# Layer-normalisation of token groups 1 to 3 moved from VectorE to GpSimd, and one subtraction per group moved the other way, in a fused cross-attention and mixture-of-experts kernel

## What is computed

```
x = x + attention(ctx, layernorm(x), Wq)          # causal, keys = values = ctx @ Wq.T
n = layernorm(x)                                  # the "second normalisation"
cw = top-2 of softmax(n @ gate_W), renormalised   # weights per token and expert
ffn = n
for e in range(8):
    ffn = ffn + cw[:, e:e+1] * (relu(n @ W1[e] + b1[e]) @ W2[e] + b2[e])
x = x + ffn
```

## Time and profile before

| | |
|---|---|
| median of 3 runs | 131.92 us (131.65 to 132.03) |
| the profiled execution | 130.83 us, of which the span from first to last instruction is 129.0 us |
| TensorE busy | 120.3 us, 93% of the span |
| VectorE busy | 107.6 us, 83% |
| ScalarE busy | 93.5 us, 73% |
| GpSimd busy | 53.5 us, 41% |
| granted TensorE clock | 1.0 (2.4 GHz) throughout |

### The profile page before, as it was taken

The page is one execution under the profiler, slowest core; times in us unless marked ns, Lnnn a source line. Parts: engine busy times, 40 slices in busy tenths (PEclk is TensorE's granted clock), DMA queues, the critical chain, the costliest instruction groups (busy, mean ns, idle before and its releaser), DMA issues. The chain is left out here.

```text
span 129.0 us, 3295 instructions
## 1 busy us (share of the span) xinstructions
PE 120.3 (93%) x1175; PEld 90.7 (70%) x1175; DVE 107.6 (83%) x419; ACT 93.5 (73%) x191; POOL 53.5 (41%) x57
## 2 busy tenths in 40 slices
PE   6987788999979999999999999999999979999991
PEld 2585566777847768778768778778776757776690
DVE  0629998989999999989898999958998798866683
ACT  3337485999776955996779927993799467989830
POOL 7199155330094951330095640330468303345400
PEclk9999999999999999999999999999999999999999
DMA  3999900000000000200000000200000002000002
GB/s 92 321 283 321 289 26 8 0 0 0 5 0 0 0 5 3 81 0 5 0 0 5 0 3 13 68 5 0 3 0 8 0 0 86 3 0 0 5 0 81
DMA packets 9904, 5.54 MB, mean 43 GB/s; under 512 B 504, under 2 KB 9888, under 8 KB 9888
## 3 DMA queue, kind: packets, MB, share of 16 engines
q1 hardware_dynamic: 9744, 5.27, 15.2%
q10 hardware_dynamic: 144, 0.07, 0.2%
HBM read 4.28 MB, written 1.05 MB: 41 GB/s over the span
## 5 line engine op out<-in xcount | busy, mean ns | idle before, releaser
L690 POOL TENSOR_TENSOR h_lo<-h,h_hi 128x512 f16<-128x512 f32 x24 | 28.7, 1196 | 40.2 <-ACT h L571 39.9
L571 ACT ACTIVATE h<-psH,b1T 128x512 f32<-128x512 f32 x64 | 43.3, 689 | 1.1 <-PE psH L508 0.9
L570 ACT ACTIVATE h_hi<-psH,b1T 128x512 f16<-128x512 f32 x48 | 33.0, 688 | 11.5 <-PE psH L387 11.4
L864 DVE SCALAR_TENSOR_TENSOR acc<-psY,weight_y,acc 128x128 f32<-128x128 f32 x125 | 35.1, 342 | 1.4 <-PE psY L408 1.2
L383 PE MATMUL psH<-x_hi,w_hi 128*128 128x512 f16 x62 | 23.5, 379 | 1.0 <-ACT h L571 1.0
L387 PE MATMUL psH<-x_lo,w_hi 128*128 128x512 f16 x62 | 23.5, 379 | 0.0
L384 PE MATMUL psH<-x_hi,w_lo 128*128 128x512 f16 x62 | 23.5, 379 | 0.0
L848 DVE TENSOR_TENSOR h_lo<-h,h_hi 128x512 f16<-128x512 f32 x24 | 16.5, 689 | 7.8 <-ACT h L571 7.3
L408 PE MATMUL psY<-w_hi,h_hi 128*128 128x128 f16 x192 | 22.7, 219 | 0.0
L408 PE MATMUL psY<-w_lo,h_hi 128*128 128x128 f16 x192 | 22.7, 219 | 0.0
L408 PEld LDWEIGHTS psY<-w_hi,h_hi 128*128 128x128 f16 x192 | 15.3, 98 | 2.2
(11 more groups left out here) (191 smaller groups left out, 191.4 us busy)
## 6 DMA issues: line engine op xcount, KB each, us to landing
w_sb<-in_L_ffn_W_dram SPq DMA_DIRECT2D x8, 256.0 KB, 4.9
out_dram<-acc SPq DMA_DIRECT2D x3, 256.0 KB, 2.3
x_sb<-in_x_dram SPq DMA_DIRECT2D x2, 256.0 KB, 4.0
ctx_sb<-in_ctx_dram SPq DMA_DIRECT2D x2, 256.0 KB, 4.4
x_sb<-in_x_dram SPq DMA_DIRECT2D x1, 512.0 KB, 7.6
ctx_sb<-in_ctx_dram SPq DMA_DIRECT2D x1, 512.0 KB, 8.5
out_dram<-acc SPq DMA_DIRECT2D x2, 128.0 KB, 1.8
wq_sb<-in_L_xattn_Wq_dram ACTq DMA_DIRECT2D x1, 64.0 KB, 2.8
```

The lines of the kernel that those rows point to most:

```text
L570: nc.scalar.activation(h_hi[:, C * (e % 2) + c, :], psH[c][:, :], ACT.Relu, bias=bias, scale=scale)
L571: nc.scalar.activation(h[:, C * (e % 2) + c, :], psH[c][:, :], ACT.Relu, bias=bias, scale=scale).then_inc(h_ready, 1)
L690: nc.gpsimd.tensor_tensor(h_lo[:, i, :], h[:, i, :], h_hi[:, i, :], ALU.subtract).then_inc(hlo0_ready, 1)
L864: last = nc.vector.scalar_tensor_tensor(out=o, in0=y, scalar=weight_y[:, g % 2, t, e:e + 1], in1=o, op0=ALU.mult, op1=ALU.add)
```

## The change

The second normalisation of groups 1 to 3 leaves VectorE's list of steps and goes into GpSimd's, directly behind the power. GpSimd no longer subtracts for expert 4 in groups 0 to 2 of the loop; VectorE takes that 128x512 subtraction ahead of its own for the same expert. TensorE waits for a count of GpSimd's remainders that fits.

```diff
+    DVE_PAIR = 4
...
+    def pool_takes(g, e):
+        return is_split(g, e) and not (e == DVE_PAIR and g < GROUPS - 1)
+
+    def pool_splits(g, e):
+        return sum(pool_takes(j, i) for j in range(g) for i in range(E)) + sum(pool_takes(g, i) for i in range(e + 1))
...
                     pe.wait_ge(hlo_ready, splits(g, e))
-                    pe.wait_ge(hlo0_ready, splits(g, e))
+                    pe.wait_ge(hlo0_ready, pool_splits(g, e))
...
             def hidden_lo0(g, e):
 
-                if is_split(g, e):
+                if pool_takes(g, e):
...
+            def loop_norm(a):
+                pool.wait_ge(rstd2_ready, (a + 1) * TG)
+                for t in range(TG):
+                    nc.gpsimd.tensor_scalar(xf[:, t, :], x1[:, t, :], mv2[:, t, 0:1], rstd2[:, t:t + 1],
+                                            ALU.subtract, ALU.mult).then_inc(xf_ready, 1)
+
+            steps = [(FIRST_RSTD, 2, first_rstd), (RSTD, 1, lambda a: attention_rstd(a, ALL)), (NORM2, 1, loop_norm),
+                     (BASE, 1, base_sum)]
...
             def hidden_lo(g, e):
+                if is_split(g, e) and not pool_takes(g, e):
+                    i = C * (e % 2)
+                    dve.wait_ge(h_ready, (g * E + e) * C + 1)
+                    nc.vector.tensor_tensor(h_lo[:, i, :], h[:, i, :], h_hi[:, i, :], ALU.subtract)
                 if is_split(g, e):
...
-                     (RESIDUAL, 1, residual_step), (VARIANCE, 1, variance_step), (NORM2, 1, lambda a: second_norm(a, ALL)),
+                     (RESIDUAL, 1, residual_step), (VARIANCE, 1, variance_step), 
```

More of the change, by code:

```diff
@@ L691, in hidden_lo0 @@
                                             ALU.subtract).then_inc(hlo0_ready, 1)
-            steps = [(FIRST_RSTD, 2, first_rstd), (RSTD, 1, lambda a: attention_rstd(a, ALL)), (BASE, 1, base_sum)]
+            def loop_norm(a):
[5 more added lines that the diff above has]
+                     (BASE, 1, base_sum)]
             def group(g):
```

## The result

The changed kernel took 133.65 us (median of 4 runs, 133.53 to 134.35) against 131.78 us for the kernel before measured with it (131.64 to 132.03): a ratio of 1.0162, interval 1.0102 to 1.0222. It is slower by about 1.6%, where no change was forecast. The time lies inside the stated range, at its dear end.

The account below looks back on a forecast made before the run. TensorE was taken to bound the kernel. Terms +0.45 (g = 0) - 0.06 - 0.06 (g = 1, 2) = +0.33 us on the median 131.92 gave 132.2 us, called no change (131.6 if GpSimd keeps the port); range 131.2 to 133.9.

Parts of the forecast that it names:

- The bound: TensorE sets the pace in the loop; at most 0.87 us of its waits can go; VectorE's saving is worth nothing by itself.
- Expert 4: TensorE's wait for the remainder of expert 4: 0.45 us gained in g = 0, 0.06 each in g = 1 and 2.
- I take 0.45: Price in us of one GpSimd normalisation: a quarter of the 128x512 tensor_scalar plus some 0.08; four cost 1.8.
- The affine select: GpSimd's 128x128 instruction nearest in shape, 0.29 us, taken to show 128 columns can be done well under half a microsecond.
- The bounds: Limits for one normalisation on GpSimd: 0.29 us (affine select of 128x128) and 1.50 us (tensor_scalar of 128x512).
- g = 1 and g = 2: GpSimd's series ends at 67.7, before TensorE loads `xf` from 68.14; expert 5's remainder just in time; -0.06 us each.
- The dear rival: GpSimd's normalisation costs 0.55 us or more; at 0.6 TensorE waits at the transposes, +1.9 us, 133.8; chance 0.32.
- g = 0: VectorE's subtraction and weight split delay GpSimd's fourth normalisation; TensorE waits 1.2 us instead of 0.75, +0.45 (-0.2 if GpSimd keeps the port).
- The cheap rival: GpSimd's normalisation costs 0.2 to 0.3 us, near the affine select; nothing is lost, gain 0.57 us, 131.3; chance 0.2.
- The third rival: VectorE's two subtractions do not hold up GpSimd's tensor_scalar, so the series runs early: 131.3; counted into a chance of 0.2.

Follow-up runs that it names:

- normalisation only: Changed kernel, but GpSimd keeps its subtraction for expert 4, ahead of its four normalisations; ratio to before 1.034.
- later power, two wide: Kernel before with GpSimd's power behind its kept expert 4 subtraction, and the normalisation as two 128x512 tensor_tensor on GpSimd; ratio to before 1.0094.
- the pair alone: Changed kernel with the normalisation back on VectorE, which still takes both expert 4 remainders in groups 0 to 2; ratio to before 0.998.
- constants: Changed kernel whose four GpSimd normalisations use 0.5 and 2.0 in place of each partition's mean and power; ratio to before 1.0055.
- two wide: Changed kernel with GpSimd's four tensor_scalar replaced by two tensor_tensor of 128x512 on all four tiles; ratio to before 1.0084.
- The durations run: Kernel before plus a series of GpSimd instructions behind its last subtraction, written to unread tiles; the change's form took 0.79 us at 128 columns.
- run with 32 columns: Changed kernel in which each of GpSimd's four normalisations writes 32 of the 128 columns; ratio to before 1.0051.

## Why the prediction was wrong

**The bound.** TensorE sets the pace: right. VectorE's time is worth nothing by itself: right only as long as VectorE is not late at the gate. Its busy time hardly moved (107.6 to 108.0 us), and the two kernels that take work from it (normalisation only; later power, two wide) still lose; but 0.14 to 1.55 us went at the gate in g = 0, to its `x_lo`, in seven of the ten other kernels of the table, and most of the gain of the pair alone went to its chain.

**Expert 4.** -0.45 us in g = 0 forecast, -0.48 measured, with 0.25 us of wait left where 0.3 was forecast; five other kernels with the pair have 0.47 to 0.49, constants 0.40, and two wide loses 0.35 instead, since GpSimd gets in between. In g = 1 and 2 about the forecast 0.06 came at the remainder, and 0.05 of it was gone again at the next hidden product, which waits for ScalarE.

**The step that failed** is "I take 0.45" for one normalisation on GpSimd. It took 0.79 to 0.80 undisturbed. I had scaled a tensor_scalar of one operation and a constant by columns and added 0.08 for the fixed part. The durations run gives 0.20 for the fixed part of that form and 0.27 for the second operation and its scalars. The affine select, from which I argued for a small fixed part, is no neighbour in kind. The bounds held it (0.29 to 1.50); the choice between them decided the sign, and the text itself said that 0.5 us was the point from which it does.

**g = 1 and g = 2.** With 0.45 nothing is lost, with the real price 0.65 each. The run with 32 columns, 0.46 us each, confirms the first (nothing lost in either). The dear rival, worked at 0.6 us, gave 0.4 a group; the measured 0.65 came at 0.79. TensorE waits at the transposes, as that rival said, and then 0.17 us more for the remainder of expert 5, which the rival did not have.

**g = 0.** +0.45 forecast for the group, +1.34 measured: the order of events was right (VectorE comes in behind the second normalisation; it was forecast behind the third, and the first is held up by 0.75), the length was not. The forecast also made VectorE wait for the normalisation in progress, and it did not (0.68 us at 39.32). And a step was missing even at 0.45: VectorE held up by GpSimd's postponed subtractions, late with `x_lo`, 0.87 us at the gate in the run with 32 columns. With the forecast's price and this step the sum would have been +1.2, and the run with those conditions gave +1.03. The right price alone, by the forecast's own scheme, is dearer still (worked under the rivals). So either error alone takes the forecast out of what it called no change.

**The rivals.** The cheap rival, 131.3, is excluded by the price. The dear one named the mechanism, the place and nearly the time (133.8); it had a chance of 0.32 and should have had more, for the reasons that stood beside it. That the time came so near is luck. Its scheme lets VectorE's subtraction for expert 5 in ahead of the fourth normalisation in g = 1, for about 0.6 us, where the rows show 0.08. Worked with the real 0.79 it gives, as an estimate, about +1.8 in g = 0 (the fourth `xf` ends at 42.36 against 40.57) and +1.2 in each of the others (69.66 against 68.49), some 4.1 us in all against 2.6 in the traces: a price too low and an interruption too many cancelled. The third rival, a tensor_scalar that VectorE's pair does not hold up, is wrong for the change's form (1.54 and 1.31 us for 0.79) and half right for the form with constants, which the second of the pair did not hold up. The rule of the Trainium skill (GPSIMD Engine Reference, Engine selection) of roughly line rate for one input does not hold for these instructions: 0.79 us for 128 columns, and 2.5 ns a column for the simplest form.

**Open.** Why a normalisation with scalars per partition waits for both of VectorE's subtractions, where one with constants or a tensor_tensor waits for the first only: the runs show the difference and not its cause. And how the 0.65 us of a group would split if one of its two waits were taken away without moving the other.

## What to carry to other kernels

A short instruction moved to GpSimd is priced by its own form, measured by a series at the end of the kernel: columns scaled from another form miss the fixed part, the second operation and the scalars. Before moving work off an engine that another waits for, look whether the waiting instruction merely stands behind one whose input comes later: putting GpSimd's subtraction ahead of the power it waited behind gave 0.5% for one number. Where GpSimd and VectorE exclude each other, price both directions for the form at hand, and follow the postponed instructions to the next place where they cross. When two waits hang on one late series, look for the one that ends last before hiding the first.

## What was not expected of the hardware

- One operand spread over the columns makes a tensor_tensor on GpSimd cheaper, not dearer: 1.04 us for 128x512 against 1.28 with two full operands, and against 2.07 for a tensor_scalar with both scalars. Two of them do in 2.1 us what four tensor_scalar do in 3.2.
- Who gets through when VectorE has two instructions in a row and GpSimd waits depends on GpSimd's form: with nearly the same moment of asking in g = 0, the normalisation with scalars per partition waited for both (1.54 us for 0.79), the tensor_tensor got in between, and VectorE's second then took 1.53 us.
- A normalisation with scalars per partition waits for VectorE's subtraction but hardly holds it up: 0.68 and 0.73 us in the change, against 1.54 beside a tensor_tensor of GpSimd.
